# Context sums of a decoder's cross-attention kept in DRAM, and the value and output products moved behind the attention loop

## The reference, cut to what matters

```python
x = x + rg_lru(layernorm(x))                            # 8 batches of 100 rows, 512 wide
lat = layernorm(x)
# cross-attention: 100 latent rows ask 722 context rows and themselves (822 keys), 8 heads of 128
xn = layernorm(ctx) * gamma + beta;  ln = layernorm(lat) * gamma2 + beta2
q = ln @ Wq + bq;  k, v = split(concat([xn, ln]) @ Wkv + bkv)
attn = softmax(q @ k.T * 128 ** -0.5)                   # per head: 100 x 822
x = x + concat_heads(attn @ v) @ Wo + bo
# router: each row goes to the best of 8 experts
h = layernorm(x);  route = sigmoid(h @ Wr + br);  e = argmax(route)
x = x + max(route) * (gelu(h @ W1[e]) @ W2[e])
```

## Time and profile before

| | |
|---|---|
| time of the runs | 1192.65 us (1191.13 to 1193.27) |
| profiled execution | 1192.44 us, of which the span is 1190.7 us |
| PE busy | 1095.6 us, 92% of the span |
| DVE, ACT, POOL busy | 760.2, 515.3, 156.3 us |
| DMA | 134.71 MB, mean 113 GB/s |
| before the batch loop's first S 2 | 0 to 224.6 us |
| one batch of the loop | 85.36 us, seven times alike |
| last batch, to the router's end | 825.0 to 906.4 us |
| choice of experts, first gather | 906.4 to 928.7 us |
| experts | 928.7 to 1190.7 us |

### The profile page before, as it was taken

One profiled execution on the slowest core, in us unless ns is written; L12 is line 12 of the kernel. 1 busy time (PEld: TensorE's weight loads), 2 busy tenths in 40 slices (PEclk: granted clock), 3 DMA queues, 4 the chain that ended last, 5 costly groups with the idle time before them and its releaser, 6 DMA issues.

```text
span 1190.7 us, 19267 instructions
## 1 busy us (share of the span) xinstructions
PE 1095.6 (92%) x6660; PEld 983.9 (83%) x6661; DVE 760.2 (64%) x1444; ACT 515.3 (43%) x949; POOL 156.3 (13%) x138
## 2 busy tenths in 40 slices
PE   3878799799999999999999999999994899999996
PEld 2857788799899899899998998998992678878775
DVE  7788616574674774675765764865426783965892
ACT  3231435334334433343334243343333673855771
POOL 6414620000000000000000000000001022211231
PEclk9988999899999999999999999999996899999999
DMA  8120466701201201202102102010016893884970
GB/s 310 40 71 28 158 212 221 263 3 57 74 0 55 74 0 55 74 0 82 48 0 82 48 5 96 28 35 15 1 37 217 282 349 132 289 306 140 342 267 28
DMA packets 72289, 134.71 MB, mean 113 GB/s; under 512 B 12205, under 2 KB 20909, under 8 KB 71232
## 3 DMA queue, kind: packets, MB, share of 16 engines
q1 hardware_dynamic: 70496, 129.49, 31.9%
q0 software_dynamic: 1760, 4.79, 1.1%
HBM read 114.57 MB, written 20.67 MB: 114 GB/s over the span
## 4 chain that ended last, share of the span: by engine, by line
PE 74%; DVE 12%; DMA 6%; issue 3%; ACT 2%; POOL 1%; SPq 1%; DVEq 0%; POOLq 0%; ACTq 0%
PE bank L533 17%; PE bank L534 17%; PE bank L535 17%; PE bank L988 6%; PE bank L995 5%; PE bank L962 3%; DMA stage<-in_W 3%; PE bank L928 2%; DVE wsl L1316 1%; DMA wo<-in_Wo_x 1%; ACT wsh L1238 1%; DMA gat<-scr_tokens,idc 1%; PE bank L949 1%; PE bank L947 1%; PE bank L980 1%
## 5 line engine op out<-in xcount | busy, mean ns | idle before, releaser
L533 PE MATMUL bank<-pt_h,xn_h 128*128 128x256 f32 (+1 forms) x576 | 169.1, 294 | 0.0
L535 PE MATMUL bank<-pt_h,xn_l 128*128 128x256 f32 (+1 forms) x576 | 163.8, 284 | 0.0
L534 PE MATMUL bank<-pt_l,xn_h 128*128 128x256 f32 (+1 forms) x576 | 163.7, 284 | 0.0
L1316 DVE TENSOR_TENSOR wsl<-stage,wsh 128x2048 fp32r<-128x2048 f32 x64 | 145.5, 2289 | 23.2 <-ACT wsh L1238 21.2
L533 PE MATMUL bank<-xt_h,qt_h 128*128 128x410 f32 (+1 forms) x384 | 140.3, 365 | 5.4 <-DMA wo<-in_Wo_x 4.5
L1238 ACT CAST wsh<-stage 128x2048 fp32r<-128x2048 f32 x64 | 122.5, 1916 | 38.1 <-DMA stage<-in_W 26.9
L534 PE MATMUL bank<-xt_l,qt_h 128*128 128x410 f32 (+1 forms) x384 | 135.2, 352 | 0.0
L535 PE MATMUL bank<-xt_h,qt_l 128*128 128x410 f32 (+1 forms) x384 | 135.1, 352 | 0.0
L1167 ACT ACTIVATE pr<-bank,smx 128x412 f32<-128x412 f32 x48 | 29.0, 604 | 226.0 <-DVE smx L1469 226.0
L533 PEld LDWEIGHTS bank<-pt_h,xn_h 128*128 128x128 f32 x576 | 108.5, 188 | 0.9
L534 PEld LDWEIGHTS bank<-pt_l,xn_h 128*128 128x128 f32 x576 | 108.7, 189 | 0.0
(11 more groups left out here) (228 smaller groups left out, 2472.9 us busy)
## 6 DMA issues: line engine op xcount, KB each, us to landing
stage<-in_W SPq DMA_DIRECT2D x64, 1024.0 KB, 7.4
scr_q<-st SPq DMA_DIRECT2D x16, 800.0 KB, 4.9
qf<-scr_q SPq DMA_DIRECT2D x8, 1600.0 KB, 6.7
raw<-in_ctx SPq DMA_DIRECT2D x8, 768.0 KB, 4.6
raw<-in_ctx SPq DMA_DIRECT2D x8, 512.0 KB
wq<-in_Wq SPq DMA_DIRECT2D x1, 2048.0 KB, 18.2
wk<-in_WkT SPq DMA_DIRECT2D x1, 2048.0 KB, 9.2
wv<-in_Wv SPq DMA_DIRECT2D x1, 2048.0 KB, 7.8
```

Of the source, the lines that this page charges most:

```text
L533: pe.matmul(dest, lh, rh, start=start and k == 0, stop=False)
L534: pe.matmul(dest, lh, rl, start=False, stop=False)
L535: last = pe.matmul(dest, ll, rh, start=False, stop=stop and k == n - 1)
L1316: return dve.tensor_tensor(dst, src, high.bitcast(F32), ALU.subtract)
```

## The change

The value and output products, the residual and the router leave the loop. In the loop ACT now copies each quarter of z to `zf` in pieces that follow the heads (7 pieces where there were 3), and at the end of each batch SP writes `zf` (1.6 MB) to DRAM (`d_z`). The loop's plan is written in another order. Behind the loop stands a new list, `tail`: 16 units, each one head for four batches. A unit is loaded from `d_z` (0.8 MB) into one of five buffers, split by ACT and DVE (`U`), multiplied by Wv in 12 float32r matmuls of 400 columns (`V`) and split again with its bias. After the 8 heads of a half come the output products of its four batches (`Y`, 24 float32r matmuls of 512 columns), each followed by residual and statistics (`A`), norm (`M`), transposes (`T`) and router product (`L`). Wv and Wo are split into high and low parts on ACT and DVE in the last batch (`WV`, `WO`); Wo is loaded in the last batch, and PE no longer waits for either ahead of the loop. The first stage loads of the expert weights stand between the loads of the units.

```diff
-    plan = [("S", 2), ("R", 0), ("B+", 0), ("PT", 1), ("N", 2), ("S", 3), ("S", 4), ("N", 3), ("R", 1), ("Z", (0,
...
+    plan = [("S", 2), ("S", 3), ("B+", 0), ("N", 2), ("PT", 1), ("N", 3), ("S", 4), ("B+", 1), ("N", 4), ("Z", (0,
...
+    splits = {("S", 2): [("WV", 0)], ("S", 3): [("WV", 1)], ("S", 4): [("WV", 2)], ("S", 5): [("WV", 3)],
+              ("PT", 6): [("U", 0)], ("Z", (2, 0)): [("U", 1), ("WO", 0)], ("Z", (2, 1)): [("U", 2), ("WO", 1)],
+              ("Z", (2, 2)): [("WO", 2), ("WO", 3)]}
...
+    tail = [("V", 0), ("U", 3), ("V", 1), ("U", 4), ("V", 2), ("U", 5), ("V", 3), ("U", 6), ("V", 4), ("U", 7),
+            ("V", 5), ("U", 8), ("V", 6), ("U", 9), ("V", 7), ("U", 10),
+            ("Y", 0), ("A", 0), ("M", 0), ("Y", 1), ("A", 1), ("T", 0), ("M", 1), ("Y", 2), ("A", 2), ("L", 0),
...
 # SP
+            def write_z(b):
+                for k in range(2):
+                    sp.wait_ge(s_zread[k], b * (ZB_USES // 2) + ZB_USES // 2 + 1)
+                sp.dma_start(d_z[b], zf[:].rearrange("p h c t -> p (h c t)")).then_inc(s_zd, 16)
+            def reload_units(js):
+                for j in js:
+                    sp.wait_ge(s_vp, j - 4)
+                    load_unit(j)
...
             with sp.Fori(0, B - 2) as b:
                 load_first(b + 2)
+                write_z(b)
+                load_begin(b + 2)
+                load_second(b + 2)
+            write_z(B - 2)
...
+            write_z(B - 1)
+            load_unit(4)
+            reload_units(range(5, 7))
+            load_weights(0, 0, range(2))
+            reload_units(range(7, 8))
+            sp.wait_ge(s_zd, 16 * (B + 1))
+            reload_units(range(8, 13))
+            load_weights(0, 0, range(2, 4))
+            for b in range(HALF):
                 finish(b)
 # PE
-                    elif what == "V":
...
+            def finish(events):
+                    if what == "V":
+                        pe.wait_ge(s_zlo, k + 1)
+                        if k >= 4:
+                            pe.wait_ge(s_otl, k - 3)
+                        split_products(
+                            pe, bank[k % 4][:, 0:HT].rearrange("p (b t) -> p b t", b=HALF),
+                            [((wv_h[:, c, h * P:(h + 1) * P], wv_l[:, c, h * P:(h + 1) * P]),
+                              (z_h[k % 3][:, :, c, :], z_l[k % 5][:, :, c, :])) for c in range(ND)], True, True
+                            ).then_inc(s_vp, 1)
                     elif what == "Y":
...
+                            pe.wait_ge(s_x2, b - 1)
+                            last = split_products(pe, zbank[b % 2][0:T, :],
+                                                  [((ot_h[:, h, cols], ot_l[:, h, cols]), (wo_h[:, h, :], wo_l[:, h, :]))],
+                                                  h == 0, h == HEADS - 1)
...
             run(0, rest)
-            pe.wait_ge(s_wb, 16 * N_WB)
             batches(pe, batch)
-            run(B, [("R", 2), ("R", 3)])
+            finish(tail)
 # ACT, in the loop and in the tail
-                        act.copy(zt[:, dc, 0:w], z[:, 0:w]).then_inc(read, 1)
+                        for h, whole, c0, c1 in segments(GROUPS[g]):
+                            if whole:
+                                last = act.copy(zf[:, h:h + whole, dc, :],
+                                                z[:, c0 - lo:c1 - lo].rearrange("p (h t) -> p h t", t=T))
+                            else:
+                                last = act.copy(zf[:, h, dc, c0 - h * T:c1 - h * T], z[:, c0 - lo:c1 - lo])
+            def high_unit(j):
+                act.wait_ge(s_zl[j % 5], 16 * (j // 5) + 16)
+                if j >= 3:
+                    act.wait_ge(s_vp, j - 2)
+                act.copy(z_h[j % 3][:], zr[j % 5][:]).then_inc(s_zh, 1)
 # DVE
+            def low_unit(j):
+                dve.wait_ge(s_zh, j + 1)
+                low(z_l[j % 5][:], zr[j % 5][:], z_h[j % 3][:]).then_inc(s_zlo, 1)
```

More of the change, by code:

```diff
@@ L82, in segments @@
     while lo < hi:
-        end = min(hi, (lo // T + 1) * T)
-        out.append((lo // T, lo, end))
+        whole = (hi - lo) // T if lo % T == 0 else 0
+        end = lo + whole * T if whole else min(hi, (lo // T + 1) * T)
+        out.append((lo // T, whole, lo, end))
         lo = end
@@ L165, in __call__, with where @@
         return t
+    def where(self, tensor):
+        return [at for t, at in self.placed if t is tensor][0]
     def over(self, other, name, shape, dtype=F32, skip=0):
-        at = [at for t, at in self.placed if t is other][0] + skip * 4
+        at = self.where(other) + skip * 4
         return self.nc.alloc_sbuf_tensor_at(name, shape, dtype, offset=at)
@@ L306, in build @@
     mem.at = base
-    late = [mem(f"stage{k}", [P, 4, FC]) for k in (2, 3)]
+    home = [mem.at + k * 4 * FC * 4 for k in range(16)]
+    wsh, wsl = [], []
+    for k, (high, low) in enumerate([(0, 1), (2, 3), (8, 13), (14, 15), (4, 5), (6, 7), (9, 10), (11, 12)]):
+        mem.at = home[high]
+        wsh.append(mem(f"wsh{k}", [P, 4, FC], F32R))
+        mem.at = home[low]
+        wsl.append(mem(f"wsl{k}", [P, 4, FC], F32R))
+    assert home[-1] + 4 * FC * 4 <= mem.where(pt_h[0])
+    stage = [mem.over(pt_h[0], f"stage{k}", [P, 4, FC], skip=k * 4 * FC) for k in range(4)]
+    mem.at = mem.where(zf)
     xg_h = mem("xg_h", [P, ND, TILE], F32R)
@@ L311, in build @@
     ht_l = [mem(f"ht_l{k}", [P, 4, TILE], F32R) for k in range(2)]
-    ohp = mem("ohp", [P, B, P])
-    stage = [mem(f"stage{k}", [P, 4, FC]) for k in (0, 1)] + late
-    assert mem.at == base_b
-    wsh, wsl = [], []
-    for k in range(8):
-        wsh.append(mem(f"wsh{k}", [P, 4, FC], F32R))
-        wsl.append(mem(f"wsl{k}", [P, 4, FC], F32R))
-    after = mem.at
+    assert mem.at <= mem.where(cqn)
+    ohp = mem.over(x1b[0], "ohp", [P, B, P])
     mem.at = raw_at
@@ L325, in build @@
     hid = [mem(f"hid{k}", [P, FC]) for k in range(2)]
-    mem.at = after
+    assert mem.at <= mem.where(mvr)
+    mem.at = tables_at
     cur = mem("cur", [P, 4])
@@ L350, in build @@
     ohs = mem("ohs", [P, B, NSLOT])
+    assert mem.at <= mem.where(zf)
+    mem.at = end_b
     ohv = mem("ohv", [P, B, 4, NSLOT])
@@ L1183, in run @@
                         g, dc = k
[L1184 removed]
                         z, read, n = zb.take()
+                        if k == (0, 0):
+                            act.wait_ge(s_zd, b * 16 + 16)
                         act.wait_ge(s_zb, n)
[L1187 to L1193 removed]
+                        lo = GROUPS[g][0] * P
@@ new lines, in high_unit, with high_weights, finish @@
+            def high_unit(j):
[3 more added lines that the diff above has]
+                act.copy(z_h[j % 3][:], zr[j % 5][:]).then_inc(s_zh, 1)
+            def high_weights(e, q):
+                act.wait_ge(s_w[q % 4], e * 32 + 16 * (q // 4) + 16)
+                act.copy(wsh[q][:], stage[q % 4][:]).then_inc(s_wh, 1)
+            def finish(events):
+                for what, k in events:
+                    if what == "V":
+                        act.wait_ge(s_vp, k + 1)
+                        h = k % HEADS
+                        if k == HEADS:
+                            act.wait_ge(s_yd, HALF)
+                        act.activation(ot_h[:, h, :], bank[k % 4][:, 0:HT], ACT.Identity, bias=bv[:, h:h + 1]
+                                       ).then_inc(s_oth, 1)
+                    elif what == "U":
+                        high_unit(k)
+                    elif what == "T":
+                        act.wait_ge(s_xtb, k + 1)
+                        act.copy(x3t[k % 2][:], tbank[k % 2][:, 0:ND * T].rearrange("p (c t) -> p c t", c=ND)
+                                 ).then_inc(s_x3t, 1)
+                    elif what == "H":
+                        act.wait_ge(s_vp, 2 * HEADS)
+                        high_weights(0, k)
```

294 lines of the change are left out of this document (166 added, 128 removed), and 19 rows, old and new, of tables (plan, tail).

## The result

The changed kernel takes 1170.3 us (median; 1169.7 to 1171.5), the kernel before 1191.9 (its three runs of above and one more): a ratio of 0.982, 95% interval 0.980 to 0.984. Predicted were 1165, 1148 to 1184, faster. The sign and the mechanism held; the gain is 22 us where 28 were forecast.

A forecast was written before the change was run, and what follows sets the result against it. PE's own work was taken to set the loop's 85.36 us period. Loop -108.8, start -7.3 and last batch with tail +88.4 sum to -27.7 us on 1192.44, giving 1165 us, range 1148 to 1184.

The forecast's parts named there:

- The two new waits of the loop: Loop: PE waits 1.6 us at S 4 for tile 2's exponentials, 0.7 at the first sum of group 2.
- those of V 4 and V 7: Tail, first half: V 4 waits about 4 us, V 7 over 6, both behind DVE and DMA.
- Last batch and tail: From the last batch to the router's end: 169.9 us where 81.5 were before, +88.4.
- the period, 67.75 + 1.6 + 0.7 = 70.05 us: Loop, each batch: 67.75 us of PE work left after 17.6 leave, plus two waits; 85.36 before.
- The last batch: Up to the first V: 54.9 us of PE work, loop waits, 4.7 at Z (0,0), 2.8 for clock; 64.7.
- The start: Ahead of the loop: PE's 4.46 us wait for Wo and 2.8 us of lowered clock go, -7.3 us.
- V 0 to 7: Tail, first half: V 7 ends at 27.9 us, plus 2.8 for the clock, 30.7; bounds 17.5 and 35.
- A: Rival: DVE's chain closes within PE's work, no waits in the loop, 14.5 us less, 1150; chance 0.15.
- C: Rival: the tail's units load at 200 GB/s instead of 359, 15 us more, 1180; chance 0.15.
- D: Rival: small waits keep the tail at the low clock, slower than before, up to 1244; chance 0.07.
- E: Rival: loop stays bound elsewhere and the tail's cost is all added, within 0.2% of before; chance 0.03.
- B: Rival: the clock falls in each batch after S 4's wait, 17 us more, 1182; chance 0.10.

The follow-up runs named there:

- the second trace: Another trace of the same changed kernel, nothing altered: 496.45 us for the seven periods, 65.67 for the last batch, 26.86 for V 0 to 7.
- the kernel with the other order: Changed kernel with X 0 to X 2 of the next batch ahead of S+ 0 and X 3 ahead of S+ 1: 1160.2 us, ratio 0.9715.

## Why the prediction was right, and where it was off

**Right.** PE's work sets the loop's period, and what leaves PE leaves the time less the waits it had covered: 17.6 us of work left, and 14.3 us a batch came off. The two new waits of the loop, the one of the last batch and those of V 4 and V 7 are where the prediction put them, for the reasons it gave; the experiments took away four of the five by moving what it had named (the fifth, for pt_l, only changed its place when it was moved). Last batch and tail were forecast to 2.0 us of 168, each piece to 2.3.

**The term that was off: the period, 67.75 + 1.6 + 0.7 = 70.05 us.** It is of the right kind and a little too small: 71.1 measured (the first 69.7 for 68.45), 7.4 us over seven periods, more than the 5 by which the whole time was missed. Two thirds of it are PE's own work, 68.42 busy for 67.75: I subtracted pieces of the chain, and took what is left to stay as it was. But the matmuls of the sums take longer than before. One of their groups, in a period of the kernel before and in one of the changed kernel:

```profile
L534 PE MATMUL bank<-pt_l,xn_h 128*128 128x256 f32 x48 | 13.4, 279 | 0.0
```

```profile
L584 PE MATMUL bank<-pt_l,xn_h 128*128 128x256 f32 x48 | 13.5, 281 | 0.0
```

Two to three ns each, 144 of them, are 0.4 of the 0.67 us. The cause stays open; the copies and the write are excluded. Another 0.3 stand in front of the two new waits, where a group of transposes runs out before PE idles instead of overlapping with the matmuls behind it. The transposes in front of S 4 take 0.93 us there, and 0.68, from their start to the start of the next matmul, in the kernel before. Before, then after:

```profile
402.49 0.93 PE L962 MATMUL bank<-ident,pr 128*128 128x128 f32 x7
403.17 0.43 PE L533 MATMUL bank<-xt_h,qt_h 128*128 128x412 f32 x1
```

```profile
370.52 0.93 PE L1046 MATMUL bank<-ident,pr 128*128 128x128 f32 x7
373.20 0.46 PE L583 MATMUL bank<-xt_h,qt_h 128*128 128x412 f32 x1 [1.75 <-ACT pr L1271]
```

(The pieces of the chain are cut where a group's last matmul ends, not where the next begins: from start to start the three value products take 8.78 us, not 8.94.) The last third are the waits, 1.77 and 0.89 for 1.6 and 0.7.

**Luck.** The last batch, 64.55 for 64.7, hits by two errors that cancel. Its waits came as forecast (7.1 us together, for 7.0), but the clock cost 1.6 for 2.8, and PE's other work took 1 us more than 54.9. In the second trace the clock did cost 2.7, and the stretch took 65.7. V 7 was to wait over 6 us and waited 2.53: the prediction had left out that the wait at V 4 lowers the clock too. V 4 to 6 took 9.2 us for 6.6. That cost nothing, since V 7 waits for its transfer, and began 24.6 us after V 0 in both traces.

**The start.** Forecast -7.3, measured -6.7 in the changed kernel from the span's start. Counted from the scores of tile 0 (208.77 before, 209.55 after), which leaves out that offset, it is -7.5. But the forecast priced the removed wait alone, and the wait moved alone gives 3.4: the other half rests on Wo's transfer leaving its place in the queue, which the prediction did not name.

**V 0 to 7.** 28.4 for 30.7. V 4 began 12.85 us after V 0 (13.0 forecast), V 7 24.6 (25.7): the terms of the queue at 359 GB/s were right to 1.1 us, and the window shows 359 again. (The bytes up to unit 7 are 7.01 MB, not 6.97, which changes none of these figures.) The 436 GB/s that the prediction set against them stand in the Trainium skill (DMA: Bandwidth & Descriptors, Anatomy of one DMA) for transfers on the path of GpSimd, and these are issued by SyncE. By that rate V 7 would have begun 3.4 earlier than forecast, at 22.3 (an estimate); the trace has 24.6.

**Rivals.** A (no waits) is excluded by the two waits; the kernel with the other order shows what it was worth, 1.4 a period. C (slow reads) by the 359 GB/s. D (tail at the low clock) by the windows: 1.00 in Y 0 to V 15, and 0.94 in Y 4 to 7, where the clock falls among the router's waits at the end, as it does in the kernel before; V 0 to 7 had 0.82. E did not occur. B, the clock falling behind the gap at S 4, was right in kind: not in the two traces of the changed kernel, but in the traces of five kernels whose loop has this gap unchanged it fell behind 7 of the 30 gaps in the loop, 1.55 us each (0 of 12 in the changed kernel). The prediction had it at 2.8 in every batch or in none.

## What to carry to other kernels

When work leaves a loop bound by one engine, the gain is that work less the waits it used to cover; follow the next engine's list by hand from event to event. Here that named all five late places ahead of the run, and left the sizes to err. Moving a read earlier moves everything behind it later: look at who stands next in the queue, and at what stands behind the waiting instruction on each in-order engine, until the chain has no one left. Here the units read early won 9 us in V 0 to 7 in three kernels, and lost all or most of it in Y 0 to V 15, first behind ACT's list and then behind the queue. They kept it when the weights, which the experts need only much later, were read behind the residual rows.

## What the runs showed of the hardware that was not expected

- The same gap does not always cost the same. PE idle for 1.76 us at S 4, after transposes: in 23 of 30 periods of those five traces the granted clock stayed 1.00 and S 4 took 4.6 us, in 7 it fell (0.64 to 0.69 over the 4 us from the start of S 4) and S 4 took 6.15. Two falls in one run lay 215 us apart in each of the three runs that had two. The Trainium skill (TensorE: Matmul & The Clock Gate, HAM oscillation) tells of waits for transfers between bursts; here waits for ScalarE and VectorE did it too.
- A shorter gap can be worse: with 1.17 us between two groups of transposes the clock fell in all seven periods, at 2.0 us a period, while 1.76 us at S 4 mostly cost no clock. So the length of a gap alone does not tell. Whether the work around it decides, or the moment at which it comes, is not shown: a gap of 1.24 us in front of transposes at the start (219.99 us in the changed kernel) left the clock at 1.00, and the seven falls, 71.7 us apart like the periods, may be one case repeated and not seven.
- Behind 3.86 us (V 4), 2.53 (V 7) and 4.65 (the last batch) the clock stood lower too: V 4 to 6 took 9.2 us, where V 0 to 2 took 2.2 each, V 7 3.8 for 2.3, and the sum behind the third 3.96 for 2.33.
- A value product of four float32 matmuls takes 2.72 us, of twelve split ones 2.26 (means of V 8 to 15, from start to start); an output product 6.87 against 5.55. The split saves 17 to 19% on TensorE and costs 1.5 us of ScalarE and 1.8 of VectorE for each unit.
